# The order of a four-layer transformer kernel laid out anew, with the gelu's waits turned round and paired maxima in layer 3

## Time and profile before

| | us |
|---|---|
| device time, median of 3 runs | 1063.44 (1061.27 to 1063.49) |
| the profiled execution: device time | 1064.05 |
| its span, first to last instruction | 1062.3 |
| TensorE busy (granted clock 0.994) | 1030.9 |
| ScalarE busy | 796.9 |
| VectorE busy | 717.8 |
| GpSimd busy | 490.7 |

### The profile page before, as it was taken

How to read it: one execution, slowest core, us unless ns; L and a number is a source line. 1 busy time by engine, 2 the same in 40 slices (tenths; PEclk the granted TensorE clock), 3 DMA queues, 4 the chain that set the end, 5 groups by cost and what they waited for, 6 DMA issues and landing times.

```text
span 1062.3 us, 19653 instructions
## 1 busy us (share of the span) xinstructions
PE 1030.9 (97%) x6697; PEld 676.1 (64%) x6697; DVE 717.8 (68%) x1479; ACT 796.9 (75%) x1344; POOL 490.7 (46%) x446
## 2 busy tenths in 40 slices
PE   7999999999999999999999999999999999999995
PEld 5788888856656656666556566566666576545442
DVE  7664748664374672355965965966956967999984
ACT  2574756598898788777787787787877778787783
POOL 2553753705446335454355436254444345445141
PEclk9999999999999999999999999999999999999998
DMA  7010000504223213122133231131212113231320
GB/s 255 11 31 20 1 21 20 128 23 116 89 53 81 61 31 78 34 61 64 38 81 81 81 95 41 32 80 51 61 31 71 31 31 86 71 81 32 90 57 25
DMA packets 36385, 64.45 MB, mean 61 GB/s; under 512 B 7208, under 2 KB 22312, under 8 KB 36288
## 3 DMA queue, kind: packets, MB, share of 16 engines
q1 hardware_dynamic: 36288, 63.20, 22.4%
HBM read 22.90 MB, written 2.12 MB: 24 GB/s over the span
## 4 chain that ended last, share of the span: by engine, by line
PE 83%; DVE 7%; ACT 3%; issue 2%; POOL 2%; DMA 1%; SPq 1%; POOLq 0%; DVEq 0%; ACTq 0%
PE AVB L660 15%; PE rings L548 15%; PE rings L550 13%; PE rings L549 13%; PE rings L647 10%; PE rings L622 6%; PE rings L591 2%; DVE m L1177 2%; PE rings L695 2%; PE rings L700 2%; POOL gT_l L1280 1%; PE rings L572 1%; PE rings L712 1%; ACT gT_h L914 1%; ACT gT_f L914 1%
## 5 line engine op out<-in xcount | busy, mean ns | idle before, releaser
L854 ACT ACTIVATE probs<-rings 128x512 f32<-128x512 f32 x592 | 315.5, 612 | 92.8 <-PE rings L647 63.1
L1177 DVE TENSOR_REDUCE m<-rings 128x1 fp32r<-128x512 f32 x512 | 318.8, 681 | 71.1 <-PE rings L622 32.8
L647 PE MATMUL rings<-SQ,SK 64*128 64x512 f32 x768 | 199.8, 439 | 2.2 <-DMA SQ<-cT 1.2
L660 PE MATMUL AVB<-probs,V 128*32 128x512 f32 x1536 | 198.9, 603 | 1.5 <-issue 1.5
L1280 POOL TENSOR_TENSOR gT_l<-gT_f,gT_h 128x512 fp32r<-128x512 f32 x96 | 120.9, 1291 | 86.8 <-ACT gT_h L914 86.8
L622 PE MATMUL rings<-SK,SQ 63*128 63x512 f32 x512 | 149.9, 437 | 1.2 <-ACT probs L854 0.4
L647 PEld LDWEIGHTS rings<-SQ,SK 64*128 64x128 f32 x768 | 92.7, 185 | 86.3 <-issue 38.4
L548 PE MATMUL rings<-w_h,gT_h 128*128 128x256 f32 x384 | 111.7, 291 | 1.9 <-DVE modb L977 1.2
L549 PE MATMUL rings<-w_l,gT_h 128*128 128x256 f32 x384 | 106.6, 278 | 0.0
L550 PE MATMUL rings<-w_h,gT_l 128*128 128x256 f32 x384 | 106.6, 278 | 0.0
L622 PEld LDWEIGHTS rings<-SK,SQ 63*128 63x128 f32 x512 | 69.8, 185 | 54.3 <-issue 16.9
(11 more groups left out here) (190 smaller groups left out, 2144.8 us busy)
## 6 DMA issues: line engine op xcount, KB each, us to landing
SQ<-qh SPq DMA_DIRECT2D x96, 128.0 KB, 2.6
SK<-kh SPq DMA_DIRECT2D x96, 128.0 KB, 2.7
SQ<-ql SPq DMA_DIRECT2D x48, 128.0 KB, 2.6
SK<-kl SPq DMA_DIRECT2D x48, 128.0 KB, 2.8
raw<-in_w SPq DMA_DIRECT2D x20, 256.0 KB, 2.8
wmod_s<-in_wmod SPq DMA_DIRECT2D x6, 512.0 KB, 5.0
gates<-gate_rows SPq DMA_DIRECT2D x12, 256.0 KB, 3.4
raw<-in_wqkv SPq DMA_DIRECT2D x9, 256.0 KB, 2.9
```

The lines of the kernel that those rows point to most:

```text
L647: mm = pe.matmul(o[:, :], SK[a % 4][r:r + KS + 1, n // 2, c * P:(c + 1) * P], SQ[a % 4][r:r + KS + 1, n // 2, :], start=True, stop=True)
L660: mm = pe.matmul(AVB[32 * n:32 * n + 32, :], V[j % 2][:, i, (HD + 1) * h:(HD + 1) * h + 32], probs[:, (4 * t + n) % PROBS, :], start=(i == ...
L854: act.activation(probs[:, n % PROBS, :], bank(kind, a, i)[:, :], ACT.Exp, scale=SCALE[layer(unit_job(a))]).then_inc(done["scores"], 1)
L1177: nc.vector.tensor_reduce(m16[:, col:col + 1], bank(kind, a, i)[:, :], AX_X, ALU.max, negate=True).then_inc(done["max"], 1)
```

## The change

Three things are changed. The waits of the gelu loop stand in another order: fc1 first, then the others. A function `paired` takes the place of the layer 1 test in `double`: exponentials are paired in layer 1, maxima in layer 3; and layer 3's max steps run in the plain order 0, 1, 2, ... while layer 2's stay at `i ^ 1`. And `TURNS` is another list, with the same steps. No operation is added or taken out but that a paired reduction replaces two.

Of `TURNS` the eighth string and the end of the last stand here; the others are changed in the same way.

```diff
+def paired(kind, u):
+
+    return layer(u // UNITS) == (1 if kind == "scores" else LAYERS - 1)
+
...
     if kind == "max":
-        return [(u, i ^ 1) for u in units[UNITS * BATCH:] for i in range(16)]
+        return [(u, i if paired("max", u) else i ^ 1) for u in units[UNITS * BATCH:] for i in range(16)]
...
-    "s C s a3 s4 h o d o3 Q s3 K s C s2 Q O K O a Z a s2 Z s4 Q2 Z p Z R p I s N2 s ld a2 s N s3 N a B q s2 M s4 a "
-    "k s2 v q k H2 s2 g K C a v g s6 f2 g4 G f2 b a s g2 lq g2 s2 K a2 g C s2 g2 wq s e g s g2 s X s a n a u2 s7 G "
-    "e f4 h s4 C r K wq d h a s lm C s3",
+    "s6 Q o4 lf s4 Z a2 s6 Q2 Z ld O2 ld Z s4 lq Q Z a R a I s4 p N p v N3 s4 K2 s2 a2 B M s4 a C a s4 v q k q H2 r "
+    "k a g s2 wq s g f2 g4 f2 G g4 a s b s2 g e g s K C s3 g a s2 g2 a s g s4 C e f2 wq f2 a u G s5 u n d s4",
...
-    "s2 m a m s3 m s o2 t o m s2 i W s m2 a o s t s2 m s m3 O2 a s2 F m4 p s m2 s K p m s m B s3 a s2 t a t m s3 m2 "
-    "s M a s2 m s2 m2 a T s m s m s m a s m2 s T s T m a m s X m s m s F s a s t s t W s5 W a s W s T s4 a s a A s6 "
-    "a s3 a3 o W o3 O2 p2 W B D2 W2 T W D2 T A T2",
+    "s2 m3 a s m2 T s3 o3 W o s3 m t a t s m s m s m2 O2 a s2 m3 p s m3 s p s m2 s4 a s3 B K m2 t2 a s m s F m3 s a "
+    "s4 M a m3 s T2 s2 T a m s2 m2 s2 m2 a s m2 s X s3 t F t W s2 a s3 a s2 W s4 W a2 s T s4 a s2 a s3 A2 a2 o W o3 "
+    "O2 p2 W B D2 W2 T W D2 T3",
...
             first = USE[(kind, a, i - i % 2)]
-            return bounded(unit_job(a)) and USE[(kind, a, i - i % 2 + 1)] == first + 1 and first % RING < RING - 1
+            return paired(kind, a) and USE[(kind, a, i - i % 2 + 1)] == first + 1 and first % RING < RING - 1
...
-                    if i == 0 and READ_BEFORE[(kind, a, i)]:
-                        act.wait_ge(pe_ring, use(*READ_BEFORE[(kind, a, i)]))
-                    if i == 1:
-                        act.wait_ge(pe_ring, use("fc2a", a, 1))
-                    elif a > 0:
-                        act.wait_ge(pe_ring, use("fc2", a - 1, 1))
-                    else:
-
-                        act.wait_ge(done["split_w1"], nth("split_w1", 0, 3))
-                        act.wait_ge(done["split_wp"], 1)
                     for m in range(i * MT // 2, (i + 1) * MT // 2):
                         act.wait_ge(pe_ring, use("fc1", a, m))
+                        if m == 0 and READ_BEFORE[(kind, a, i)]:
+                            act.wait_ge(pe_ring, use(*READ_BEFORE[(kind, a, i)]))
+                        if m == MT // 2:
+                            act.wait_ge(pe_ring, use("fc2a", a, 1))
+                        elif m == 0 and a > 0:
+                            act.wait_ge(pe_ring, use("fc2", a - 1, 1))
+                        elif m == 0:
+
+                            act.wait_ge(done["split_w1"], nth("split_w1", 0, 3))
+                            act.wait_ge(done["split_wp"], 1)
```

## The result

The changed kernel takes **1044.93 us** in the median of four runs (1044.23 to 1046.05), the kernel before beside it 1062.87; the ratio is 0.9834, with a 95% interval of 0.9817 to 0.9852. The forecast was 1051.5 us. The time lies in the range, 6.6 us under the forecast.

What follows compares the result with a forecast made beforehand. It took a chain of TensorE's steps, lengthened by slow readers, as the bound, with VectorE the bound from 900 to 1020 us. Terms -4 -1 -4 -3 = -12 us gave a forecast of 1051.5 us, range 1037 to 1067.

Steps and rivals of the forecast that it cites:

- maxima: Layer 3: merged two-bank maxima shorten VectorE's work where it is the bound; 4 us saved (bounds 2.7 and 6.0).
- exponentials: Layer 1: the new order merges 100 pairs of exponentials for 88, saving ScalarE 1 us.
- gelu: Gelu loop: table loads run while TensorE still makes fc1; 4 us saved (bounds 0 and 9.9).
- order: New step list: more steps between producers and TensorE's next need in layer 1; 3 us saved (bounds 0 and 4.9).
- I take 100, the middle, for 42 pairs: Maxima of layer 3: each merged pair saves 100 ns, between 64 and 142, giving 4.2 us of VectorE.
- Three places stand out: New order's changed distances: layer 1's normed q and k (3 us), a shift row (nothing), layer 3's shift product (rival).
- The stall of layer 1: Last job of layer 1: TensorE ran dry and its clock fell; 4.9 us lost, 3 us taken as gain.
- The shift rows: First unit of layer 1's last job finds its shift row later; taken as nothing (bounds 0 and 1.2 us).
- (a): Rival, slower: TensorE stands before layer 3's shift product; 1073 or 1069 us, deciding from 8 us on; chance 0.16.
- (b): Rival, no change, 1063 us: TensorE's waits are only moved, or merging undoes itself by holding banks; chance 0.14.
- (c): Rival, much faster, 1030 or 1041 us: much of the 31 us behind maxima and all gelu waits go; chance 0.15.
- what was to show the prediction right: Gelu table loads hardly idle, 63 merged reductions of 1.14 to 1.25 us, no layer 1 clock drop, VectorE's maxima stretch shorter.

Runs made afterwards that it cites:

- e4: The changed kernel with the gelu loop's waits put back as they were before; 1053.08 us, ratio 0.9898.
- e5: The changed kernel with layer 3's maxima each read singly again, plain order kept; 1045.51 us, ratio 0.9841.
- e7: The kernel before with only layer 3's maxima in plain order, none merged; 1072.18 us, ratio 1.0093.
- h1: The kernel before with only the first 103 steps of the new order; 1061.83 us, ratio 0.9984.
- h2: The kernel before with the new order up to layer 2's first maximum (820 steps), old waits and swapped maxima; 1054.50 us, ratio 0.9922.
- e3: The kernel before with only the new order of steps; layer 3's maxima swapped and unmerged, gelu waits old; 1058.79 us, ratio 0.9960.
- h3: The kernel before with the new order only from layer 2's first maximum on, layer 3's maxima plain and unmerged, old gelu waits; 1064.22 us, ratio 1.0004.
- e9: The kernel before with one local edit in layer 1's last job, transposed q and k placed seven steps later; 1062.35 us, ratio 0.9982.
- e8: The changed kernel without merging and with layer 3's maxima back in swapped order; 1049.63 us, ratio 0.9875.
- e1: The kernel before with only the gelu loop's waits turned round; 1058.51 us, ratio 0.9958.

## Why the prediction was right, and where it was wrong

**The sum was right in sign and too small; two of its terms were too small, and one does not exist.** It said -4 (maxima) -1 (exponentials) -4 (gelu) -3 (order). The runs give about 0, not tried apart, -4.5 alone and -6.7 to -9.0 in the new order, and -10.9 for the order with plain, merged maxima (e4). The gelu and the order with its maxima make up the change: 10.9 + 6.7 = 17.6. That the sum came within 6.6 us is in part luck: the order gave what the maxima did not.

**The maxima: the step that failed is "I take 100, the middle, for 42 pairs: 4.2 us of VectorE where it is the bound".** The merged reduction's own length was right, 1220 ns foreseen and 1219 measured, though it was drawn from two reductions of different memories. Of the 42 pairs put in VectorE's full stretch, 34 start between 880 and 1000 us. Where they follow closely a pair gives the next instruction way 1.14 us after its start, where two single ones take 1.20:

```profile
908.15 1.23 DVE L1174 TENSOR_REDUCE m<-rings 128x2 fp32r<-128x1024 f32 x1
909.29 2.10 DVE L1177 TENSOR_REDUCE m<-rings 128x1 fp32r<-128x512 f32 x3
...
914.00 2.48 DVE L1177 TENSOR_REDUCE m<-rings 128x1 fp32r<-128x512 f32 x4
```

That is 0.06 us less, the lower bound of 64 ns. But not even this is left in the sum (319.7 us for 319.3), because the single maxima that remain stand more loosely: 632 ns of busy time each (244.0 over 386), 624 in e5. The premise failed too: in that stretch VectorE was nearly full, yet TensorE's slots set the time as much, as e7 shows. The Trainium skill (Perfetto Trace Analysis, "Optimizing Scalar/DVE Operations") lets grouping help where the engine is saturated, and puts an overhead of some 125 ns on each VectorE instruction on PSUM; where the engine isn't saturated but causes bubbles on others, it lets breaking up help. Here a pair saves 0.06 us at best and neither effect shows in the time, e5 and the changed kernel being the same.

**The gelu waits: right.** Mechanism, sign and size were as said (4 foreseen, 4.5 alone). That the term is larger in the new order was not. The view of waiters accounts for it; why the new order exposes the gelu more I did not settle.

**The order: the step that failed is "Three places stand out", after which 3 us of the one stall were taken for the whole order; e4 measured 10.9.** The stall of layer 1 was rightly found and rightly priced within its bounds (3 of at most 4.9; 4.3 in the table). What I left out is the start (1.7 us by h1), where the clock drop stood in the trace of before, and nearly 3 us that the list gains between 61 and 344 us, a little at a time (h2: 2.3 to 5.2, while h1 stays where it was); which of its moves do that was not tried.

A sentence beside it does not hold as a reason: "It holds the same 2446 steps, 1883 of them on the ring, so TensorE's work is the same". How many score products run two at a time depends on which heads stand side by side, up to 67 slots or 10 us in these lists. That the new list with plain maxima comes to 670 slots for 669 is not something the prediction had looked at; with swapped maxima it is 708, and the order alone gives 4.3 us then (e3).

**The shift rows: right.** Their wait fell instead of rising. **The rivals.** (a), TensorE before the shift product, was to decide from 8 us on; it is 5.7. Its count was misread: 163 and 128 are TensorE's steps behind maximum 15, but in the old order maximum 14 is a unit's last. Behind the last one they go from 122 to 128, so that nothing moved closer. (Of the same kind is a slip in the maxima: the old order's last three strings hold 167, not 159; no term hangs on it.) (b), waits only moved, holds for h3 and in part for e9, but not for the whole. (c) came half true: a third of the 31 us behind the maxima is gone, and the waits for the gelu's banks went from 13.1 to 5.4, not to nothing. Of what was to show the prediction right, the table loads, the merged length and the clock came as written; VectorE's stretch of maxima did not become 3 to 6 us shorter.

No run beat the changed kernel. e5, without the merging, is as fast and simpler.

## What to carry to other kernels

Where matmuls use only half of the rows, the order of heads decides how many of them run in pairs: count the slots of the written order, not its steps, and choose the order within a unit together with the order of the steps. Put the wait that comes last first in the code, so that a table load runs while it is waited for. Test a part both ways, alone in the old kernel and taken out of the new one: e7 and e8 give the same order of maxima opposite signs.

## What the runs showed of the hardware

Two score products of 64 and 63 rows on different halves started at the same time (940.28), two of the same half 0.23 us apart (931.41 and 931.64, in e7). A reduction over two banks takes 1219 ns and gives way after 1.14 us, which saves 0.06 us on two of 681 ns when they follow closely, and nothing in the sum here. Idling 1.76 us at the start was followed by the lower granted clock, 1.2 GHz, and a fold of 3.68 us instead of 1.89. VectorE's normalisation of one tile of tokens took 1.37 us beside a GpSimd operation (at 107.57 before) and 0.35 with none there (at 101.72 after). Of several waits before an activation that needs a table load, the one first in the code stayed with the activation: 12.5 us of waiting before 22 loads became 2.1 (e1).
